# Gated edge stage of a graph network: attribute tiles 4 and 5 of each step on partitions 64 to 127, with weights of their own

## What is computed

```python
src, dst = edge_index[0], edge_index[1]
concat = jnp.concatenate([h[src], h[dst], edge_attr], axis=-1)   # 96 + 96 + 64 columns
gates = jax.nn.sigmoid(concat @ W_e + b_e)
messages = jax.nn.softplus(concat @ W_n + b_n)
h_new = jax.ops.segment_sum(gates * messages, dst, num_segments=n)
return h + h_new / edge_count
```

## Time and profile before

| | |
|---|---|
| median of 3 runs | 3197.06 us (3196.53 to 3200.12) |
| span of the profiled execution, first to last instruction | 3184.9 us |
| gated edges, first to last addition L1174 | 1295.09 to 2551.51 us of the span |
| PE / PE weight loads / DVE / ACT / POOL busy, whole span | 84 / 75 / 53 / 43 / 28 % |
| granted clock of TensorE, mean of the span | 0.752 |

### The profile page before, as it was taken

How to read it: one execution, slowest core, us unless ns; L and a number is a source line. 1 busy time by engine, 2 the same in 40 slices (tenths; PEclk the granted TensorE clock), 3 DMA queues, 4 the chain that set the end, 5 groups by cost and what they waited for, 6 DMA issues and landing times. The chain is left out here.

```text
span 3184.9 us, 66445 instructions
## 1 busy us (share of the span) xinstructions
PE 2666.3 (84%) x21196; PEld 2393.9 (75%) x21197; DVE 1691.5 (53%) x3605; ACT 1361.4 (43%) x2809; POOL 905.6 (28%) x1144
## 2 busy tenths in 40 slices
PE   3888889869999998788878888888878769859999
PEld 2777778759999996666666666666666657649999
DVE  7877787773444436544444444444444452355555
ACT  2444444423333334344444444444444431207776
POOL 2111211200000000566655666566656600000000
PEclk7999999979999998555555555555555559878999
DMA  2333333320000002444434444443434360028272
GB/s 68 115 101 100 104 115 102 103 76 2 2 2 2 2 2 75 121 107 103 103 101 102 106 103 103 101 106 102 104 101 103 101 243 24 1 88 348 92 260 78
DMA packets 221040, 300.38 MB, mean 94 GB/s; under 512 B 101187, under 2 KB 186662, under 8 KB 215430
## 3 DMA queue, kind: packets, MB, share of 16 engines
q1 hardware_dynamic: 181926, 217.20, 21.6%
q0 software_dynamic: 38880, 79.68, 10.3%
HBM read 225.96 MB, written 70.80 MB: 93 GB/s over the span
## 5 line engine op out<-in xcount | busy, mean ns | idle before, releaser
L1130 POOL DMA_INDIRECT layer_R<-source_terms,layer_srcs x804 | 764.0, 950 | 500.0 <-DVE layer_zp L1174 275.5
L1332 PE MATMUL layer_zp<-layer_Wa,layer_at 64*128 64x192 f32 x1620 | 606.7, 538 | 244.4 <-issue 242.5
L1332 PEld LDWEIGHTS layer_zp<-layer_Wa,layer_at 64*128 64x128 f32 x1620 | 488.1, 322 | 308.4 <-issue 301.4
L536 PE MATMUL build_win<-nodes_x,build_S 128*128 128x200 bf16 x5264 | 501.4, 253 | 125.2 <-DVE nodes_x L453 117.2
L536 PEld LDWEIGHTS build_win<-nodes_x,build_S 128*128 128x128 bf16 x5264 | 442.7, 99 | 180.1 <-DVE nodes_x L453 116.8
L931 PE MATMUL layer_acc<-layer_U,graph_CT 128*128 128x192 f16 x6250 | 521.4, 247 | 19.0 <-DVEq L761 19.0
L931 PEld LDWEIGHTS layer_acc<-layer_U,graph_CT 128*128 128x128 f16 x6250 | 517.3, 98 | 26.5 <-issue 22.7
L1174 DVE TENSOR_TENSOR layer_zp<-layer_zp,layer_R 128x1152 f32<-128x1152 f32 x135 | 183.7, 1361 | 399.4 <-remote 399.4
L1282 ACT ACTIVATE layer_y<-layer_zp 128x1152 f32<-128x1152 f32 x135 | 152.6, 1130 | 472.7 <-DVE layer_zp L1174 439.9
L1356 PEld LDWEIGHTS layer_acc<-layer_hot,layer_G 128*98 128x98 f32 x1644 | 287.3, 288 | 38.0 <-issue 35.5
L1356 PE MATMUL layer_acc<-layer_hot,layer_G 128*98 128x32 f32 x1644 | 292.6, 349 | 15.1 <-DVE layer_G L1186 5.0
(11 more groups left out here) (243 smaller groups left out, 2873.9 us busy)
## 6 DMA issues: line engine op xcount, KB each, us to landing
layer_ring<-W_blocks SPq DMA_DIRECT2D x41, 1600.0 KB, 7.7
W_blocks<-nodes_x SPq DMA_DIRECT2D x400, 100.0 KB, 1.8
layer_at<-in_attr SPq DMA_DIRECT2D x135, 192.0 KB
C_blocks<-build_Cblk SPq DMA_DIRECT2D x25, 800.0 KB, 3.5
layer_C<-C_blocks SPq DMA_DIRECT2D x25, 800.0 KB, 21.4
layer_rows<-target_rows SPq DMA_DIRECT2D x135, 144.0 KB
layer_R<-source_terms,layer_srcs POOLq DMA_INDIRECT x804
layer_Qs<-target_terms SPq DMA_DIRECT2D x135, 36.0 KB
```

The source lines that it names most:

```text
L536: mm = pe.matmul(out, S[:, b, part, 2 * i + u, :, :].rearrange("p a z -> p (a z)"), M[:, i, u, :, :].rearrange("p a z -> p (a z)"), start= ...
L1130: nc.gpsimd.indirect_dma_start(R[:, h, u, :], None, P_d, bass.IndirectOffsetOnAxis(ap=at_u, axis=0)).then_inc(s_R[h], 16)
L1332: mm = pe.matmul(out[u], at[:, h, u * P:(u + 1) * P], Wa[:, :], start=(u % 2 == 0), stop=False, skip_group_check=True)
```

## The change

`Wa` gets 128 partitions: the 64 rows of weights are loaded twice, to partitions 0 to 63 and to 64 to 127 (four small loads in place of two). `at` gets 128 partitions and four tiles of columns (LOWER = 4): tiles 0 to 3 of a step lie on partitions 0 to 63, tiles 4 and 5 on partitions 64 to 127, by two loads in place of one. The attribute products run in the order 0, 4, 1, 5, 2, 3, each on the half of the partitions on which its tile lies. Semaphore counts are adapted. Nothing else is changed.

```diff
+LOWER = 4
-        Wa = m.sb("Wa", [DE, D2], F32)
+        Wa = m.sb("Wa", [P, D2], F32)
-        at = m.sb("at", [DE, 2, SE * P], F32)
+        at = m.sb("at", [P, 2, LOWER * P], F32)
...
-            sp.dma_start(Wa[:, 0:D], We[2 * D:, :]).then_inc(s_wa, 16)
-            sp.dma_start(Wa[:, D:], Wn[2 * D:, :]).then_inc(s_wa, 16)
+            for half in (slice(0, DE), slice(DE, P)):
+                sp.dma_start(Wa[half, 0:D], We[2 * D:, :]).then_inc(s_wa, 16)
+                sp.dma_start(Wa[half, D:], Wn[2 * D:, :]).then_inc(s_wa, 16)
...
-                sp.dma_start(at[:, h, :], attr[:, bass.ds(s * (SE * P), SE * P)]).then_inc(s_at[h], 16)
+                sp.dma_start(at[0:DE, h, :], attr[:, bass.ds(s * (SE * P), LOWER * P)]).then_inc(s_at[h], 16)
+                sp.dma_start(at[DE:P, h, 0:(SE - LOWER) * P],
+                             attr[:, bass.ds(s * (SE * P) + LOWER * P, (SE - LOWER) * P)]).then_inc(s_at[h], 16)
...
-            dve.wait_ge(s_wa, 48)
+            dve.wait_ge(s_wa, 80)
...
-            pe.wait_ge(s_wa, 48)
+            pe.wait_ge(s_wa, 80)
...
-                pe.wait_ge(s_at[h], turn * 16 + 16)
-                for u in range(SE):
-                    mm = pe.matmul(out[u], at[:, h, u * P:(u + 1) * P], Wa[:, :], start=(u % 2 == 0), stop=False,
+                pe.wait_ge(s_at[h], turn * 32 + 32)
+                for u in (0, 4, 1, 5, 2, 3):
+                    half = slice(0, DE) if u < LOWER else slice(DE, P)
+                    c = u % LOWER * P
+                    mm = pe.matmul(out[u], at[half, h, c:c + P], Wa[half, :], start=(u % 2 == 0), stop=False,
                                    skip_group_check=True)
```

## The result

| | before | after |
|---|---|---|
| median of five runs each | 3198.03 us (3196.53 to 3200.24) | 3210.22 us (3206.88 to 3215.33) |
| ratio, 95 % interval | | 1.0039 (1.0028 to 1.0050) |
| span of the profiled execution | 3184.9 us | 3213.6 us |
| gated edges, first to last addition | 1256.42 us | 1279.90 us |

The change makes the kernel slower by 12 us, 0.39 %. The profiled execution of after took 3215.33 us, the slowest of its five. A run takes 1.7 to 1.9 us more than its span in every run whose span is on record, so the profiled execution of before, with 3184.9 us, is about 10 us shorter than the five runs of before beside it.

The account below looks back on a forecast made before the run. Bound: POOL's burst of gathers and its tail, 18.90 us for two steps. Span 3184.9 + 0.6 us for the `Wa` loads (products and second load 0) = 3185.5, with 12.2 around it 3197.7 us; range 3112 to 3240.

Parts of the forecast that it names:

- The bound: Gated edges: POOL's burst and tail set each pair of steps, 1.64 + 13.81 + 3.45 us, 18.90 us in all.
- The argument from the stage's third step: Gated edges: PE is 4.28 us behind there, yet the release comes only 0.12 us later, so it is counted from POOL.
- The attribute group: PE's twelve attribute matmuls (L1332) in a step: from 4.20 us to 2.9 to 4.2 us, taken at 3.0.
- Worth on the path 0: The shorter attribute products on PE gain 0, hidden by DVE's 2.09 us wait for ACT and by the late signal.
- The two more loads of `Wa`: Once, on SP before the first `rows` and `at`: cost 0 to 1.2 us, taken at 0.6 us.
- The second load hidden: SP's extra load of `at` in each step: its 0.78 us is hidden before the consumers, cost 0.
- The second rival: Split load lengthens POOL's tail through more pieces in the DMA queues: 3208 to 3270 us, taken at 3225; chance 0.18.
- The first rival: PE's work sets the release in the gated edges: 3114 or 3149 us, taken at 3130, or 2943 us; chance 0.27.
- Its second form: The release follows the start of PE's next attribute group: 0.73 us a pair, 49 us in all, 3149 us.
- The time around the span: Before and after the profiled span: 12.2 us, added to the span to get the run's time.

Follow-up runs that it names:

- four_gathers: The kernel before with the gathers of tiles 4 and 5 left out from the third step on; 2881.89 us, ratio 0.9009.
- two_loads: The kernel before with the attribute load of each step cut in two, everything still on partitions 0 to 63; 3275.5 us, ratio 1.0246.
- one_load: The kernel after with attributes laid out beforehand, so one padded load of 128 partitions brings all six tiles; 3195.5 us, ratio 0.9980 to the kernel before.
- idle_load: The kernel before with one more load in each step, into a buffer that nobody reads; 3345.95 us, ratio 1.0457.
- second profile of before: Profile of the kernel before with an added POOL wait (`s_ms`, s + 1) that holds nothing; 3202.38 us, ratio 1.0004.

## Why the prediction was right or wrong

- *The bound: right.* The stage is the burst of gathers and its tail. All parts measured as read: gaps of 6.29 and 12.6 to 12.9 us, 1.64 us from the addition to the first gather (1.64 measured), 13.81 us to the last one (13.84), and a release that ignores TensorE: with the attribute group 1.28 us shorter it comes later after TensorE's work by more than that (8.18 to 9.64 us in the pairs shown). `four_gathers` settles it, with TensorE's work unchanged and 316 us less. The argument from the stage's third step was sound. The semaphore times of before say it directly: of the products that end at 2116.39 and 2117.47 the semaphores were set at 2124.47 and 2124.54.
- *The attribute group: right.* 2.9 to 4.2 us with 3.0 taken, 2.92 measured. (The working has a slip: (4.20 - 0.52) / 11 is 0.335 us and not 0.32. The recorded starts are 0.48 us apart once and then 0.32, and eight of them are left, as reckoned.) It holds for the group behind the short gap alone; the other is stretched by the standstill and gained nothing. TensorE's busy time fell by 153.6 us where up to 170 was said. The rule that a weight load overlaps a running matmul only across row groups (the Trainium skill, TensorE: Matmul & The Clock Gate, "Packing small matmuls — row/col tiling") would give the one row group 10.3 us before the change; it took 4.20, and the halves took it to 2.92 us, so they do add overlap and the one row group had most of it already. The same section also allows a load into the background weight buffer to be pulled ahead, which the 4.20 us agree with. Without the alternation it is 3.09 us, so the order is no condition.
- *Worth on the path 0: nearly.* With one load, the halves save 0.20 % (0.11 to 0.29 %), 6.5 us. The mean tail falls from 3.62 to 3.47 us, less than the 0.21 us between two profiles of before. The cause of this small gain isn't shown. With two loads they are worth 65 us, and this the prediction did not see: TensorE's lead keeps the aggregation at 3.55 us into the burst in place of 5.7, so DVE's waits for its signal stay short. L1199 waits 48.7 us in after against L1196's 388.8 us in `two_loads`.
- *The two more loads of `Wa`: 0.6 us taken, 0 measured.* From SP's first load of `Wa` to the first addition it is 17.72 us before (1277.37 to 1295.09) and 17.73 us after (1281.55 to 1299.28).
- *The second load hidden: wrong, and the step that failed.* I followed `rows` and `at` to their consumers and found cover in the middle pairs. It costs 14.7 us by the medians, 19 by the ratios, 16.5 us in the stages of the traces. At the stage's start the products do wait for `at`, 2.76 us, where I had taken the distance of one earlier load as enough; that is 4.1 us. The other part is 0.19 us for each of 66 pairs, in the tail, without anyone waiting for the data.
- *The second rival is what happened, at its low end.* It gave 0.16 us for each pair from the share of more pieces in the tail, 3208 us; 0.19 us and 3210.22 us were measured. The size fits by luck, for the mechanism (the number of pieces in the DMA queues) is refuted. The trace of before records 48 packets for a gather, 576 in a pair, and 610 for its plain loads, not the 1536 and 512 pieces of the prediction. `one_load` has 126 plain packets more in a pair than before and no longer tail, after has 158 more. By the same reckoning `two_loads` would cost 10 to 72 us and costs 75, and `idle_load` 144. I gave this case 0.18 and should have given it more: a tail whose cause the trace doesn't show is no ground on which to cost another transfer at nothing.
- *The first rival is refuted*, in all its forms: with the products faster, the release kept its distance to POOL. Its second form, the start of the next group, also had that group wrong, which stands half done when the release comes.
- *The time around the span: wrong.* I took 12.2 us for what lies before and after it. In the run of after it is 3215.33 - 3213.6 = 1.7 us, and 1.7 to 1.9 us in the other profiled runs. The profiled execution of before was a faster one than those behind its median. On three chips of this study the kernel before took 3200, 3202 and 3189 us, and on the last its spans were 3183.9 to 3188.6 us; whether the profile comes from such a chip isn't on record. Between its two profiles the difference lies in the stage (1256.42 and 1270.54 us), in the tail (3.41 and 3.62 us).

What stays open: why the signals of TensorE are held in the later part of a long burst of gathers; what in one more plain load makes the tail longer, now that `one_load` clears its bytes and its packets; and why the tail differs by 0.2 us between profiles of the same program. The packets narrow it down. The last gather's packets end 2.3 us after its start in all of these kernels; what grows is the time from there to the signals, in which no gather packet moves: 1.1 us in before and 1.2 in `one_load`, 1.3 in the second profile of before and in after, 1.4 in `two_loads`, 1.5 in `idle_load` (medians).

## What to carry to other kernels

Where a wait is named "remote" and the producer had long been done, ask what else had just ended: count the release from every engine, in the one step where they differ. If gathers hold the signals, less work for the producer is worth little unless it brings a signal out of the held part of the burst (there it was worth 65 us); one more small load is dear even if its data are early, and the cheapest remedy is on the gathering engine: let it wait for the held signal and start from there (one line, 1.5 % here; 1.8 % with the halves and one load). A load split for the sake of a layout should be made whole by laying the data out for it.

## What the runs showed of the hardware that was not expected

- In a burst of twelve gathers, signals of TensorE's products that end in its first 3 us come out within 0.02 us. Of those that end 6 to 15 us into it, nine in ten come out 3.2 to 3.8 us after the start of the last gather, 1.1 us behind the last gather packet in before. The gathers' own signals come out in the middle of the burst.
- While its signals are held, TensorE comes to a standstill too: twelve matmuls that wait for nothing between them spread over 6.5 us in place of 3.7 in before.
- A load of 65 KB that nobody reads costs 1.07 us in each of 135 steps (144 us); SP's record of it is 0.47 to 0.71 us long.
- Two halves of partitions at work together take a group of twelve float32 matmuls from 4.20 to 2.92 us, and to 3.09 us when only one of the five changes from tile to tile within a step goes from half to half.
- The same program was 0.4 % faster on one chip than on two others, as much as this change is worth.
